# A cross-attention kernel's opening: value units moved from behind the first queries to directly behind the key units

## What is computed

```python
x = x + xattn(layernorm(x), ctx, mask, Wq, Wk, Wv, Wo)     # 16 heads of 32; 512 queries against 8192 keys per batch
x = x + attn(layernorm(x), Wq_amp, Wk_amp, Wq_phi, Wk_phi, Wv, Wo, score_log_scale)
x = x + ffn(layernorm(x), w_router, w_fc, w_gate, w_proj)  # 16 experts, top 2
```

```python
q = (layernorm(x) @ Wq)    # then split into heads
k = context @ Wk
v = context @ Wv
attn = softmax(where(mask, q @ k.T * scale, -max))
out = (attn @ v) @ Wo
```

## Time and profile before

| what | us |
| --- | --- |
| median of 3 runs | 1930.38 |
| fastest and slowest of them | 1928.66, 1931.12 |
| profiled execution, its own time | 1917.37 |
| its span, from the first to the last instruction | 1915.6 |
| PE busy, share of the span | 96% |
| DVE busy | 89% |
| ACT busy | 76% |
| mean granted clock of TensorE | 0.992 |

### The profile page before, as it was taken

How to read it: one execution, slowest core, us unless ns; L and a number is a source line. 1 busy time by engine, 2 the same in 40 slices (tenths; PEclk the granted TensorE clock), 3 DMA queues, 4 the chain that set the end, 5 groups by cost and what they waited for, 6 DMA issues and landing times.

```text
span 1915.6 us, 56880 instructions
## 1 busy us (share of the span) xinstructions
PE 1841.6 (96%) x24652; PEld 812.1 (42%) x24652; DVE 1706.8 (89%) x1530; ACT 1457.6 (76%) x1660; POOL 45.9 (2%) x57
## 2 busy tenths in 40 slices
PE   8999999999999998999999999999998989998895
PEld 4444444444444443334444444444442445556431
DVE  6899999999999999979999999999998588788655
ACT  2699999999988987869998888989987465555121
POOL 2000000000000000000000000000000000001103
PEclk9999999999999999999999999999999999999998
DMA  8333333333333333322333333333333000005795
GB/s 262 119 95 100 105 98 101 106 106 106 101 95 98 99 84 101 111 68 78 90 101 84 84 90 90 96 90 96 89 79 122 24 1 1 2 1 207 245 307 165
DMA packets 113773, 196.21 MB, mean 102 GB/s; under 512 B 10352, under 2 KB 64624, under 8 KB 113520
## 3 DMA queue, kind: packets, MB, share of 16 engines
q1 hardware_dynamic: 110528, 183.33, 32.6%
q0 software_dynamic: 2560, 8.39, 1.3%
q10 hardware_dynamic: 432, 0.79, 0.1%
HBM read 109.63 MB, written 50.33 MB: 84 GB/s over the span
## 4 chain that ended last, share of the span: by engine, by line
PE 40%; DVE 40%; issue 15%; ACT 3%; DMA 1%; POOL 1%; DVEq 0%; POOLq 0%; SPq 0%; ACTq 0%
DVE dacc L1881 31%; PE ps L1217 8%; PE ps L1464 7%; PE ps L1116 4%; PE ps L1113 4%; PE ps L1306 3%; PE ps L1244 2%; DVE wsm L1824 2%; DVE wsm L2203 2%; PE ps L1346 2%; PE ps L1201 2%; PE ps L1269 2%; PE ps L1153 1%; PE ps L1301 1%; PE ps L1315 1%
## 5 line engine op out<-in xcount | busy, mean ns | idle before, releaser
L1733 ACT ACTIVATE pt<-ps,bias 128x1024 f32<-128x1024 f32 x1024 | 1096.9, 1114 | 182.0 <-PE ps L1464 99.2
L1881 DVE TENSOR_TENSOR dacc<-dacc,pt 128x2048 f32<-128x2048 f32 x496 | 1135.0, 2288 | 42.9 <-ACT pt L1733 16.2
L1464 PE MATMUL ps<-qst,kst 128*32 128x512 f16 x8192 | 620.7, 380 | 12.1 <-ACT pt L1733 10.1
L1217 PE MATMUL ps<-pt,vt 128*32 128x512 f32 x4096 | 485.1, 592 | 0.0
L1464 PEld LDWEIGHTS ps<-qst,kst 128*32 128x32 f16 x8192 | 211.6, 97 | 367.1 <-issue 153.4
L1116 PE MATMUL ps<-wsm 128*32 128x512 f16 x4608 | 314.9, 380 | 0.0
L1113 PE MATMUL ps<-wsm 128*32 128x512 f16 x4464 | 305.7, 379 | 0.0
L1217 PEld LDWEIGHTS ps<-pt,vt 128*32 128x32 f32 x4096 | 123.9, 110 | 211.0 <-issue 145.7
L1116 PEld LDWEIGHTS ps<-wsm 128*32 128x32 f16 x4608 | 125.4, 97 | 125.7 <-issue 3.2
L1113 PEld LDWEIGHTS ps<-wsm 128*32 128x32 f16 x4464 | 120.8, 97 | 121.0 <-issue 2.0
L1824 DVE SCALAR_TENSOR_TENSOR wsm<-ps,wsm 128x512 f16<-128x512 f32 x126 | 86.0, 683 | 8.1 <-ACT wsm L1549 8.0
(11 more groups left out here) (229 smaller groups left out, 1231.2 us busy)
## 6 DMA issues: line engine op xcount, KB each, us to landing
kst<-kscr SPq DMA_DIRECT2D x132, 256.0 KB, 3.5
kscr<-wsm SPq DMA_DIRECT2D x126, 256.0 KB, 3.5
kst<-kst SPq DMA_DIRECT2D x124, 256.0 KB, 3.4
wsm<-in_ctx SPq DMA_DIRECT2D x31, 768.0 KB, 5.3
wx<-in_gate SPq DMA_DIRECT2D x10, 512.0 KB, 8.2
wx<-in_fc SPq DMA_DIRECT2D x10, 512.0 KB, 9.5
wx<-in_proj SPq DMA_DIRECT2D x10, 512.0 KB, 9.2
qst<-qscr SPq DMA_DIRECT2D x32, 128.0 KB, 3.2
```

The source lines that it names most:

```text
L1217: p = e.matmul(ps[32 * h:32 * h + 32, 4 + n % 2, :], vt[:, kb % 2, ch, c:c + 32], pt[:, (2 * i + h // 2) % 6, h % 2, :], start=ch == 0, st ...
L1464: p = e.matmul(ps[r:r + 32, 2 * half + h2, :], kst[:, kb % 2, h, ch * 128 + r:ch * 128 + r + 32], qst[:, h, :], start=True, stop=True)
L1733: e.activation(pt[:, (2 * i + half) % 6], ps[:, 2 * half:2 * half + 2, :], ACT.Exp, bias=bias[:, 4 * kb + ch:4 * kb + ch + 1], scale=SCORE ...
L1881: e.tensor_tensor(own_heads, own_heads, probs, ALU.add).then_inc(S["add"], 1)
```

## The change

The value units of block 0 are multiplied directly behind the key units, ahead of the first turned tiles. They take banks 0 to 3, those of the turned rows, instead of turns in banks 6 and 7, and each of the turned tiles 0 to 3 now waits until the value unit in its bank has been evicted. The value weights are loaded ahead of the first rows and split on DVE ahead of the rows' statistics. ACT evicts the four keys and units 4 and 5 ahead of the first root, and units 6 and 7 behind it.

```diff
@@ bank_users
-    for u in (0, 1, 4, 5, 6, 7):
+    for u in (0, 1):
         unit(0, u)
@@ unit_bank
-    return 4 + u % 2 if kb == 0 and u in (2, 3) else 6 + BANK_OF[kb, u] % 2
+    if kb == 0 and u > 1:
+        return 4 + u % 2 if u < 4 else u - 4
+    return 6 + BANK_OF[kb, u] % 2
@@ sp
             for c in range(3):
                 e.dma_start(wraw[:, 0, c], A["wk"][128 * c:128 * c + 128, :]).then_inc(S[f"in{c}"], 16)
+            e.dma_start(wraw[:, 1], A["wv"].rearrange("(k p) n -> p k n", p=128)).then_inc(S["wv"], 16)
             e.dma_start(xs[:, 0:4, :], A["x"][0:512, :].rearrange("(t p) c -> p t c", p=128)).then_inc(S["x0"], 16)
             e.dma_start(wq[:], A["wq"].rearrange("(k p) n -> p k n", p=128)).then_inc(S["wq"], 16)
-            e.dma_start(wraw[:, 1], A["wv"].rearrange("(k p) n -> p k n", p=128)).then_inc(S["wv"], 16)
@@ pe
             def whole(u):
-                unit(0, u, 0, 9, bank((0, u)))
+                unit(0, u, 0, 9, unit_bank(0, u))
@@ pe, turned
                     e.wait_ge(S["n1"], t + 1)
-                    if t > 3:
+                    if t < 4:
+                        e.wait_ge(S["vev"], t + 1)
+                    else:
                         e.wait_ge(S["xTc"], t - 3)
@@ pe
             first_keys()
+            for u in range(4, 8):
+                whole(u)
             e.wait_ge(S["const"], 1)
             turned(range(4))
             e.wait_ge(S["wq"], 16)
             for g in range(4):
                 queries(0, g)
-            for u in range(4, 8):
-                whole(u)
             turned(range(4, 8))
@@ act
+            for u in FIRST_KEYS + (4, 5):
+                evict(0, u)
             root(rs[:, 0:4], ve[:, 0:4], "var", 1, "root")
-            evict(0, 2)
-            evict(0, 3)
+            for u in (6, 7):
+                evict(0, u)
             turned(range(4))
-            evict(0, 0)
-            evict(0, 1)
             root(rs[:, 4:8], ve[:, 4:8], "var", 2, "root")
-            for u in range(4, 8):
-                evict(0, u)
             turned(range(4, 8))
@@ dve
+            wsplit()
             normal(range(4), 0)
             for u in FIRST_KEYS:
                 k_low(0, u)
             queries(0, 0)
-            wsplit()
             queries(0, 1)
             queries(0, 2)
             normal(range(4, 8), 1)
```

## The result

The changed kernel takes 1934.55 us by the median of 22 executions, against 1930.04 of the kernel before (also 22): a ratio of 1.0024, with a 95% interval of 1.0017 to 1.0031, that is 3.3 to 6.0 us more. The forecast was 1933.4 in a range of 1929.2 to 1936.8. A second timing of the same pair gave 1.0012 (1.0001 to 1.0023), about 2.3 us.

The account below looks back on a forecast made before the run. TensorE (PE) works for 96% of the span, so the opening's gain or loss reaches the end one for one. Order +1.65 us and clock 1.4 made +3.1: 1930.38 + 3.1 = 1933.4, range 1929.2 to 1936.8.

Parts of the forecast that it names:

- The order: Opening up to the second turning: moving the units alone costs +1.65 us, 2.20 of idle gone, 3.93 new, 0.08 in joints.
- value units: On PE directly behind the first keys: run from 13.84 to 21.72 with no idle time ahead of them.
- queries: First queries on PE start at 24.54 against 18.94, 5.60 us later, where the moved work is 7.88.
- second statistics: DVE's statistics of the second rows, behind the third queries as before: start at 36.44.
- the stall: New PE idle time of 3.9 us ahead of the second turned tiles, released by DVE's normalization.
- the second turning: PE's transposes of the second four row tiles start at 42.37 instead of 40.72.
- The clock: Behind PE's new idle time ahead of the second turned tiles the clock falls: 1.4 us, bounds 0 and 3.4.
- rival 2: Low clock behind the new idle time lasts for the long case: price 3.44, total +4.3 to +5.1, 1935.1; chance 0.18.
- Rival 1: Clock holds through PE's new idle time ahead of the second turned tiles: +1.65, 1932.0; chance 0.20.
- The first queries' way back: First queries' trip to HBM and back ahead of the scores: 1.3 us left, cost 0, bounds 0 and 1 us.
- the query weights: Transfers in the opening: query weights and everything behind them land as before, at 12.84.
- a chance of 0.31: Total slower than 1934.2, a change of 0.2% (3.9 us): the long low clock mostly (0.18), a quarter of the forecast (0.13).

Follow-up runs that it names:

- split: Changed kernel with the second rows' moments on DVE moved ahead of the first queries' split, root and normalization behind it; ratio to the kernel before 0.9998, first scores at 63.12.
- halved: Changed kernel with only value units 4 and 5 behind the keys, units 6 and 7 back behind the first queries; ratio to the kernel before 0.9991, first scores at 62.75.
- warm: Changed kernel with 15 unused 128x512 float16 products in PE's new stall ahead of the second turned rows; ratio to the kernel before 1.0011, first scores at 66.12.
- delay: Kernel before with 12 unused 128x512 float16 products on PE ahead of the first unit of block 1; ratio to the kernel before 1.0000, first scores at 68.14.
- after_3: Changed kernel, unchanged, a single further execution; first scores (start of the steady loop's first scores) at 70.20, rest of the span 1860.1 us.
- before_again: Kernel before, unchanged, a single further execution; first scores (start of the steady loop's first scores) at 66.39, rest of the span 1851.8 us.
- after_2: Changed kernel, unchanged, run again on the same chip as three other repeats; first scores at 67.56, rest of the span 1867.3 us.

## Why the prediction was right

**The order.** Each of these steps came out within 0.25 us of its forecast, given in brackets: value units 13.67 to 21.62 (13.84 to 21.72), queries at 24.41 (24.54), second statistics at 36.32 (36.44), the stall 3.78 (3.9), the second turning 42.16 (42.37), +1.44 for +1.65. `split` and `halved` show that this is the cause and not only a fit: giving the second rows their moments earlier, or leaving two units in front of them, removes the stall, and then the opening is faster than before, by 1.3 and 1.7 us.

**The clock.** Taken at 1.4 us; 1.15 in the first profile, as `warm` confirms. But as a mean over executions the term was mis-sized on both sides. Three executions of the changed kernel give 2.2, with one at 4.0 (rival 2's price of 3.44, exceeded), and the kernel before, for which the prediction took none ("the granted clock stays at 1.00 through the opening with its idle 2.20 us"), loses 1.2 on the average of five. First scores are at 68.3 on average after (three) and at 65.7 before (five, taking `delay` without its 2.24 us of products): 2.5 us apart. The sentence in which one quiet execution stood for the rule was the weak one. That the net share still comes out near the forecast (2.2 less 1.2 is 1.0, for 1.4) is luck: two errors cancel. Rival 1 (the clock holds) was not seen in three executions.

**Transposes and the clock.** In the first profile the low stretch ends before the queries, in `after_3` it runs through turned rows, maxima and most of a query product. The Trainium skill's sentence on transposes (TensorE: Matmul & The Clock Gate, Part 4: PE-mode transpose) would have them keep the clock low. Three traces speak against it for the 128x128 float32 transposes of this kernel: in `delay`, `before_again` and `after_2` the clock came back while the sixteen transposes of the turned rows were all that PE had done since it fell. In `after_2` it was 0.50 from 42.60 to 45.60, 0.72 from there to 45.90 and 1.00 behind that, and this is PE's row:

```profile
42.34 3.62 PE L1146 MATMUL ps<-ident,xn 128*128 128x128 f32 x16 [3.78 <-DVE xn L1819]
```

In `before_again` it was 0.50 from 16.50 to 19.50 and 0.67 from there to 20.00, with the turned rows from 16.40 to 20.00. Why it stayed down three times as long in `after_3` is not shown.

**The transfers.** The first queries' way back was not the limit of the changed kernel, as forecast, but with more to spare than the sum left. SP's timeline of the changed kernel:

```profile
36.83 2.52 SPq L897 DMA_DIRECT2D qst<-qscr  x4
```

The loads moved by 3.0 us (from 33.82), not by the 4.3 of the keys' low halves. In `split` they were issued at 37.16 and there at 42.23, so here at about 41.9, and PE asked at about 45.0: some 3 us to spare, not 1.3. `split` asks 3.9 us earlier and loses 1.17. DVE split the value weights from 9.83 on and the rows' moments began at 12.54 (9.5 and 12.2 forecast). One reading of the prediction is wrong and cost nothing: the query weights do not land as before, since the value weights now stand ahead of them too. They landed at 3.3 + 12.0 = 15.3, 2.5 us later, for a use at 24.41.

**The total.** The measured 1934.55 is in the range, 1.15 over the forecast and just over 1934.2, where the prediction had put a chance of 0.31. The openings account for about 2.5 us on average, but that hangs on three values between 67.0 and 70.2 and five between 64.4 and 67.3. The second timing agrees (1.0012, 2.3 us); the first (3.3 to 6.0 us) asks for at least 0.8 more, which the spread of the openings alone could hold. Some of it may lie in the low stretch near 1550 us. From the first scores to DVE's first copy of turned keys behind it (`KT`) it is 1495.8 to 1496.9 in the five profiles of the old order and 1496.5 to 1497.3 in the three of the changed kernel, 0.6 apart on average; that is no more than their spread. The rest of the span shows no order by kernel on one chip (1862.9 and 1862.7 before, 1867.3 and 1860.1 after), but with a scatter of 7 us it can't exclude 2. So it isn't shown where the remainder of the first timing lies, or whether it is chance. Why the rest differs by chip wasn't tried.

## What to carry to other kernels

Before moving work ahead into a gap, ask what it covers where it stands: here 7.9 us of units filled a gap of 2.2 and uncovered one of 3.8, because another engine's queue still did its part in the old order. Either split the work in proportion to the two gaps, or move the other engine's work into its own idle time first. And where PE stands still for 2 us or more, one profile is not enough to say what the clock does.

## What was not expected of the hardware

- The same idle time of about 2 us on PE brought the clock to its 1.2 GHz level in some executions and not in others of the same order: nothing lost twice, then 1.6, 1.7 and 2.8 us (and nothing behind the 2.01 us of `split`, in another order). The low stretch behind one stall of 3.78 us lasted 3.4 us in one execution of the changed kernel and, at a mean of 0.53 over 11 us, over 10 in another. And in three executions it ended while PE did transposes alone.
- One program differs by some 10 us of 1930 from chip to chip (the kernel before: medians of 1917.3, 1927.3 and 1930.5), and the profiles part between about 1750 and 1800 us, where the expert weights are loaded. What the 4.5 us steps in the chain are wasn't tried. Two profiles from two chips say nothing there about a change of 3 us.
